# Local attention on one core: TensorE takes the products of two quads in one visit, from rings of seven, and GpSimd makes 40 of 88 products in place of 42

## The reference, cut to what matters

```
J offsets = 0..40, 96, 128, 384          # 44 keys for each query
k_mod  = k[t - offset_j] * (1 + scale_embed[j])          # per head, 16 numbers
scores[h, t, j] = sum_d q[h, t, d] * k_mod[h, t, j, d] / 4 + pos_bias[j, h]
attn   = softmax over j (offsets that reach before the start are masked)
out[t] = (sum_j attn[h, t, j] * v[t - offset_j]) * gain  @ w_out
x = x + out
```

## Time and profile before

| | us |
|---|---|
| median of the 3 timed runs | 2227.41 |
| lowest, highest | 2201.74, 2236.6 |
| the profiled execution's own time | 2204.41 |
| its span, first to last instruction | 2202.6 |
| TensorE, VectorE, ScalarE, GpSimd busy | 2035.4, 1887.8, 1500.3, 764.5 |

### The profile page before, as it was taken

One profiled execution on the slowest core, in us unless ns is written; L12 is line 12 of the kernel. 1 busy time (PEld: TensorE's weight loads), 2 busy tenths in 40 slices (PEclk: granted clock), 3 DMA queues, 4 the chain that ended last, 5 costly groups with the idle time before them and its releaser, 6 DMA issues. The chain is left out here.

```text
span 2202.6 us, 41807 instructions
## 1 busy us (share of the span) xinstructions
PE 2035.4 (92%) x14402; PEld 682.5 (31%) x14402; DVE 1887.8 (86%) x2195; ACT 1500.3 (68%) x3579; POOL 764.5 (35%) x1019
## 2 busy tenths in 40 slices
PE   7899999999997869999999999999999999999888
PEld 5445545455543322122122121222222122222133
DVE  3697888888876759999999999999999999999445
ACT  0255666666653318888888888888888888888831
POOL 2599999999994108002012011020000000051200
PEclk9999999999998669999999999999999999999999
DMA  8466576566656415001011010010000000041321
GB/s 283 127 132 131 112 169 146 128 162 149 143 131 141 95 49 116 15 20 37 4 29 28 3 40 18 4 49 8 6 23 4 6 23 4 6 121 31 109 71 57
DMA packets 228751, 161.11 MB, mean 73 GB/s; under 512 B 152808, under 2 KB 199864, under 8 KB 228584
## 3 DMA queue, kind: packets, MB, share of 16 engines
q1 hardware_dynamic: 198272, 112.61, 21.2%
q0 software_dynamic: 14944, 31.33, 5.5%
q10 hardware_dynamic: 15376, 14.93, 2.1%
HBM read 97.64 MB, written 44.11 MB: 64 GB/s over the span
## 5 line engine op out<-in xcount | busy, mean ns | idle before, releaser
L1418 DVE TENSOR_REDUCE mx<-ps_m 128x2 f32<-128x1024 f32 x980 | 1155.3, 1221 | 52.4 <-PE ps_m L1295 33.0
L1404 ACT ACTIVATE pr<-ps_s 128x512 f32<-128x512 f32 x2048 | 1063.8, 602 | 195.2 <-PE ps_s L1323 195.1
L1323 PE MATMUL ps_s<-qs,ks 50*128 50x512 f16 x2048 | 618.2, 383 | 18.4 <-ACT pr L1404 10.8
L1339 PE MATMUL ps_o<-pr,vg 128*32 128x512 f32 x4096 | 546.4, 605 | 0.2 <-ACT pr L1404 0.2
L1295 PE MATMUL ps_m<-ks,qs 48*128 48x512 f16 x1960 | 474.4, 384 | 70.2 <-DVE mx L1418 40.7
L584 POOL TENSOR_TENSOR room<-qs 128x512 f32<-128x512 f32 x336 | 414.3, 1266 | 79.4 <-ACT qs L851 54.7
L1252 POOL DMA_DIRECT2D vg<-vb_d x24 | 19.6, 819 | 1059.0 <-PE ps_o L1339 978.5
L1323 PEld LDWEIGHTS ps_s<-qs,ks 50*128 50x128 f16 x2048 | 154.3, 94 | 619.6 <-ACT pr L1404 612.8
L923 DVE TENSOR_TENSOR room<-PSa,qs 128x512 f32<-128x512 f32 x368 | 234.0, 678 | 13.2 <-PE PSa L677 12.7
L677 PE MATMUL PSa<-room,sj 128*32 128x512 f32 x1408 | 196.8, 606 | 7.7 <-DVE room L923 2.8
L1295 PEld LDWEIGHTS ps_m<-ks,qs 48*128 48x128 f16 x1960 | 99.9, 93 | 288.6 <-DVE mx L1418 237.3
(11 more groups left out here) (162 smaller groups left out, 1895.0 us busy)
## 6 DMA issues: line engine op xcount, KB each, us to landing
room<-skew SPq DMA_DIRECT2D x128, 208.0 KB, 3.9
skew<-attn SPq DMA_DIRECT2D x64, 164.0 KB, 4.6
tail_room<-in_W SPq DMA_DIRECT2D x32, 256.0 KB, 3.5
tail_room<-in_W2T SPq DMA_DIRECT2D x32, 256.0 KB, 4.5
vb_d<-vb SPq DMA_DIRECT2D x8, 1024.0 KB, 6.0
qs<-ks SPq DMA_DIRECT2D x26, 256.0 KB, 5.3
ks<-k_d POOLq DMA_DIRECT2D x48, 128.0 KB, 3.2
qs<-q_d POOLq DMA_DIRECT2D x180, 32.0 KB, 2.8
```

The costliest lines, as they stand in the source:

```text
L1323: pe.matmul(ps_s[:, op % SB, :], ks[rows, slot, j // 2, kt * P:(kt + 1) * P], qs[rows, q, j // 2, :], start=True, stop=True).then_inc(s_ps, 1)
L1339: mm = pe.matmul(ps_o[SLOT * j:SLOT * (j + 1), :], vg[:, kt, j, :], pr[:, kt % 4, j, :], start=(kt == 0), stop=(kt == KT - 1), skip_group_ ...
L1404: act.activation(pr[:, kt % 4, j, :], ps_s[:, op % SB, :], ACT.Exp, scale=exp_scale).then_inc(p_ready, 1)
L1418: dve.tensor_reduce(mx[:, :, pair * TILES + tile, quarter], ps_m[:, u % 2, :, :], AX_X, ALU.max).then_inc(m_read, 1)
```

## The change

`in_pairs` goes through TensorE's list. The products of an even quad are held back and issued right before those of the next odd quad, so that both are one visit. The other steps keep their order. Rings have 7 buffers in place of 6 and are tensors of their own. POOL_SHARE falls from 42 to 40, so VectorE makes 48 products; which of the 88 they are shifts too.

```
-POOL_SHARE = 42
+POOL_SHARE = 40
 ON_POOL = [(k * POOL_SHARE) % len(PRODUCTS) < POOL_SHARE for k in range(len(PRODUCTS))]
-RING = 6
+RING = 7
+def in_pairs(order):
+    out, held = [], []
+    for place in order:
+        if place[1] != "products":
+            out.append(place)
+        elif place[2] % 2 == 0:
+            held.append(place)
+        else:
+            out += held + [place]
+            held = []
+    return out
-        room = sb("room", [P, 16384], F32)
+        room = sb("room", [P, 10240], F32)
-        prod_d = room[:, 1024:4096].rearrange("p (k n) -> p k n", k=RING)
-        prod_p = room[:, 4096:7168].rearrange("p (k n) -> p k n", k=RING)
+        prod_d = sb("prod_d", [P, RING, CH], F32)
+        prod_p = sb("prod_p", [P, RING, CH], F32)
...
-            for j, what, i in order_of(PE_STEPS, PE_LAST):
+            for j, what, i in in_pairs(order_of(PE_STEPS, PE_LAST)):
```

More of the change, by code:

```diff
@@ L361, in local_stage @@
         v64 = q_room[:, 4864:6912].rearrange("p (k c n) -> p k c n", k=TILES, c=KC)
-        room = sb("room", [P, 16384], F32)
+        room = sb("room", [P, 10240], F32)
         rope_a = room[:, 0:512]
         rope_b = room[:, 512:1024]
-        prod_d = room[:, 1024:4096].rearrange("p (k n) -> p k n", k=RING)
-        prod_p = room[:, 4096:7168].rearrange("p (k n) -> p k n", k=RING)
-        own = room[:, 7168:9216].rearrange("p (a h s) -> p a h s", a=2, h=8)
-        v96 = room[:, 9216:11264].rearrange("p (k c n) -> p k c n", k=TILES, c=KC)
-        xh = room[:, 11264:12288].rearrange("p (k n) -> p k n", k=KC)
-        sc = room[:, 12288:15360].rearrange("p (k n) -> p k n", k=KC * len(BANKS))
-        qparts_last = room[:, 12288:13312].bitcast(F16).rearrange("p (a s n) -> p a s n", a=2, s=PARTS)
-        a0 = room[:, 15360:16384].rearrange("p (h t) -> p h t", h=8)
+        prod_d = sb("prod_d", [P, RING, CH], F32)
+        prod_p = sb("prod_p", [P, RING, CH], F32)
+        own = room[:, 1024:3072].rearrange("p (a h s) -> p a h s", a=2, h=8)
+        v96 = room[:, 3072:5120].rearrange("p (k c n) -> p k c n", k=TILES, c=KC)
+        xh = room[:, 5120:6144].rearrange("p (k n) -> p k n", k=KC)
+        sc = room[:, 6144:9216].rearrange("p (k n) -> p k n", k=KC * len(BANKS))
+        qparts_last = room[:, 6144:7168].bitcast(F16).rearrange("p (a s n) -> p a s n", a=2, s=PARTS)
+        a0 = room[:, 9216:10240].rearrange("p (h t) -> p h t", h=8)
         tail_room = sb("tail_room", [P, 4096], F32)
```

## The result

| | before | after |
|---|---|---|
| median of the executions timed together, us (4 each) | 2228.7 | 2282.27 |
| lowest, highest | 2201.74, 2236.6 | 2279.53, 2285.42 |
| the profiled execution's own time | 2204.41 | 2279.53 |
| its span | 2202.6 | 2277.7 |

The ratio is 1.0282, with a 95% interval from 1.0191 to 1.0374: the change makes the kernel slower by 2.8%. I had forecast 2242, with 2270 as the high end. The medians differ by 53.6 us, the two profiled executions by 75.1. So 75 us is what the change costs between executions of like kind.

A forecast was written before the change was run, and what follows sets the result against it. TensorE was taken to bound the middle blocks, GpSimd and VectorE the first. Waits of 32.7 us, less 7.3 of gain and 1 from the first two blocks, made +24 on the mean of 2217.5: 2242 us, range 2203 to 2270.

The forecast's parts named there:

- Gain: TensorE, middle blocks: four fewer runs of narrow matmuls (24 to 20) at 0.33 us each save 1.3 us a block.
- t_mean1: TensorE waits 1.8 us for t_add, late behind Q3's products held for Q0's buffers, in six blocks.
- values: TensorE waits about 1.8 us for VectorE's rotation, late behind Q15's products held for Q12's buffers, in five blocks.
- t_mean0: TensorE waits 1.05 us for t_add, late behind two products held for Q18's buffers, in six blocks.
- Cover: Quads moved from ahead of qk0, k0 and ffn expose waits of 0.6 (six blocks), 0.4 and 0.2 us (five).
- The second rival: Waits also drop TensorE's clock, about 1.7 us a fall, 19 us more, giving 2261; chance 0.13 with longer chains.
- The two products for VectorE: Moving two products from GpSimd costs VectorE 1.4 us a block, hidden beside slower TensorE: nothing in middle blocks.

The follow-up runs named there:

- e2: Changed kernel with pairs kept, VectorE's ring at 9 buffers and GpSimd's at 6 in place of 7 each; ratio to the kernel before 1.0006.
- e5: Changed kernel with only the share undone: GpSimd makes 42 of 88 products again, pairs and rings of seven stay; ratio to the kernel before 1.0106.
- e12: Changed kernel with VectorE, ScalarE and SyncE lists reordered, needed steps ahead of held products, only the last rotation ahead of Q16's; ratio to before 1.0136.
- e8: Changed kernel with turn2 and turn7 making their eight transposes three times over in each block but the last; ratio to the kernel before 1.0276.
- e1: Changed kernel without in_pairs: old order on TensorE, rings of 7, 40 products on GpSimd; ratio to the kernel before 0.9969.
- e10: Changed kernel with VectorE, ScalarE and SyncE lists reordered, h_center and both late rotations ahead of Q15's products; ratio to the kernel before 1.0190.

## Why the prediction was wrong

The direction was right, and so was the first cause, held buffers that stop VectorE's list; the size was not: + 24 us forecast, + 75 in the profiled executions (+ 54 between the medians). For blocks 2 to 6 the forecast's terms make 22.8 us and the trace has 60.4. Of the 37.6 between them 13.7 are the clock, which the sum put at nothing; 9.2 are the gain, which did not come (6.5 forecast, 2.7 more work found); 9.2 are the waits at turn5 and, in block 6, h_mean, which it did not have; 2.9 is logits6; the waits that it had are together 2 us longer than forecast (31.3 against 29.3), and 0.6 are small waits. By its steps:

- **"Gain: 4 x 0.33 = 1.3 us a block", so 7.3 in all: this term failed.** TensorE's work in a block went from 77.20 to 77.61 (e2), 77.88 (e5), 77.86 (e12), all at full clock: 0.4 to 0.7 more, and why it is more stays open. The 0.33 was measured where a visit stands between 512-column matmuls. Most of the moved quads stood beside short transposes or pv. Q12 was between pv5 and logits0: from the start of pv5's last two matmuls (L764, 411.29) to the first of h_mean (413.94) it took 2.65 us, and without it, in e2, 1.84. That is 0.8 less, no more than its own streaming of 0.86, which it costs again in its pair. The count of narrow runs was right; at this place the price was not found. That it belongs to one kind of neighbour is my reading of these two places, no run changed the neighbours alone.
- **t_mean1, "1.8": 2.44.** Held products, update and TensorE's arrival came within 0.15 us as computed; t_add took 1.47, not 0.73.
- **values, "1.8": 2.18.** The delay was reckoned from h_center at h_mean + 1.63, read in one block of before. In the three others it is + 1.17, so that the held products move it by 2.2 us, not 1.76. That 1.8 is only 0.4 off comes from the one row.
- **t_mean0, "1.05": 1.34 in that block, 0.78 in the others.** T_add took 1.50 us there and 0.94 elsewhere, against the 0.69 of the earlier trace rows; TensorE, too, came some 0.6 later than computed, so that less than the difference shows, and mostly less than the forecast.
- **Cover, "0.6" at qk0, "0.4" at k0, "0.2" at ffn:** 0.53, 0.31 and under 0.1. Logits6 was left out and is 0.5.
- **Which waits there are.** I went through the steps that TensorE takes directly from VectorE. Turn5 is reached from VectorE over SyncE's queue and over ScalarE's list; both were there to be followed (the earlier trace rows is that very place) and I did not. It is 1.9 us in that block, 1.5 on the mean of the five, and 1.8 more at h_mean in block 6.
- **The second rival was at work.** "Mine are 1.8, between full stretches, so it is unlikely": two of the waits were over 2. Falls cost 13.7 us in five blocks; e8 removes most of them by adding work. The rival had the right price (1.7 each), and idle times near 2 us are indeed where falls begin in these traces; it had too low a chance, since my bound on the waits was from the one value of each step and took no slower step in.
- **The two products for VectorE, "nothing there".** Nearly true without pairs (e1, at most 0.9 us a block). With pairs it is 5.3 us a block (e5): where VectorE stands behind a held buffer its time is not free, a product less there also kept t_add (t_mean1's) clear of GpSimd's products, and the shorter waits brought no fall.

The sum again for blocks 2 to 6, measured: idle 44.0, clock 13.7, more work 2.7 us, together 60.4. The forecast for five blocks was (1.8 + 1.8 + 1.05 + 0.6 + 0.6 - 1.3) x 5 = 22.8.

The base, too, was a mean of executions between 2202 and 2237; the profiled ones, 2204.41 and 2279.53, differ by 75.1, and their rest beyond the local stage is of the same kind in both. The forecast's mean of 2217.5 thus held executions with the long fall, while by their clocks those of after have none. That makes the miss look smaller: 40 us from 2242 to the median of 2282, but 51 from 2228, on the profiled base, to 2279.5.

## What to carry to other kernels

To use a buffer later is to hold every in-order engine that fills the ring, and what waits is whatever stands behind the next fill in its list, also two queues on; list the consumers of each such step over all engines before pricing the waits. Put what others wait for ahead of a fill that can block: that took back nine of twelve us a block here, with no buffer added. And read a base from several blocks: one of the five here was unlike three of the others. The price of a switch may belong to its neighbours: read it at the place from which the step is moved and at the place to which it goes.

## What the runs showed of the hardware

**Falls of TensorE's clock behind short waits.** In the fourteen traces I set each idle stretch of TensorE of 0.9 us or more, between 120 us and block 7, against the falls of the clock beside it. Of 91 stretches under 1.7 us none has one, of 37 from 1.7 to 2.1 us six, of 52 from 2.1 us on 37. A fall here lasts 3.4 us at half clock and costs 1.7 us; four of the 43 last 6.8. In 162 of the 180 stretches TensorE was busy over 90% of the three us on either side. So a wait of 1.0 us costs 1.0, and one of 2.4 us costs 2.4 and most times 1.7 more.

**VectorE beside GpSimd.** The adds of two SBUF operands, 128 x 512 (t_add and the rotation's), take 0.69 us where GpSimd does nothing (41 in the local stages of the fourteen traces), 0.69 to 0.92 beside its small 128x128 steps (far; 174), and 0.69 to 1.79, with a median of 1.40, where they lie under its products (200). In before, up to 620 us, t_add on t_xm mostly fell between GpSimd's products, eleven of twelve at 0.69 to 0.92; in after nine of ten lie wholly under its products, three at 0.93 or 0.94 and six at 1.47 to 1.50. It is not so every time: in e12 five stand at 0.69 beside such a span, though GpSimd's spans are rough. VectorE's products, one operand of which is in PSUM, stay at 0.68 (L923, L937). The held rings make both engines start at the same event, and so t_add on t_xm went from 0.73 to 1.26 us on the mean. The Trainium skill (SBUF — State Buffer, Who interferes with whom) has it that a VectorE instruction with two SBUF inputs contends with a GpSimd instruction that reads SBUF, and one with at most one SBUF input, outside the two-port modes, does not. The traces agree with the second half, a steady 0.68; with the first beside GpSimd's products, though 19 of the 200 adds show under 0.8 us there, and only faintly beside its small steps, which read SBUF too.

**One long fall sets the spread between executions.** What follows the local stage took 1384.7 to 1391.6 us in eight of the fourteen profiled executions and 1401.0 to 1407.4 in six, whatever the kernel. The long ones have one stretch at half clock, of 61.4 us (47.8 in e10), near the end of the full attention, here in e5, and then the same place of the program in before:
```profile
2104.40:2165.80 61.40, 57.41 (x207) 7.27 (x207) 10.71 (x10) 33.68 (x65) 8.71 (x14) 0.50 0.31 97
```
```profile
2065.70:2127.10 61.40, 48.19 (x259) 13.84 (x258) 19.70 (x23) 37.53 (x72) 8.68 (x14) 0.97 0.32 108
```
For 61.4 us TensorE stayed at 1.2 GHz though it was busy 57.41 of them; the same part of before ran at full clock but for one short fall, 0.97 on the mean. That makes some 20 us. It fits the executions without a trace too: of 52 of before, measured beside the experiments, the 14 from 2201.5 to 2212.8 us have a mean granted clock of 0.970 to 0.975, and the 38 from 2215.5 to 2234.9 have 0.957 to 0.964. The four of after (0.963 to 0.966, its profiled one without the long fall at 0.966) are too close together for one to have it and another not. What decides whether it comes was not tried. It is why the trace's local stage tells more here than a ratio.
